# First attention of a four-layer kernel: scores of 16 heads in one block of 32-row products, and one maximum over two banks

## The chip, the cores and the metric

The kernel runs on one core of one Trainium2 chip. The metric is the device time of one execution in microseconds (us), the median of the runs. The engines are named as in the profile: PE is TensorE, PEld its weight loads, DVE VectorE, ACT ScalarE, POOL GpSimd, SP SyncE.

## The reference, cut to what matters

The input x has 16 sequences of 128 positions and 128 channels. Four layers follow, each with a conditioned projection, an attention (or a recurrence), a second conditioned step and a feed-forward part. The change touches the attention of the first layer alone:

```
y   = x @ (W_base + 2 * sum_e cond[b, e] * Bs[e] @ As[e]).T + b_base
Q,K = y @ Wq.T, y @ Wk.T          modulated per channel by amplitude and phase
V   = (y + y shifted by one position) @ Wv.T, modulated per channel
for each of 16 heads (8 channels each):
    scores = (cos part of Q . cos part of K + sin part of Q . sin part of K) * 8 ** -0.5
    out    = softmax(scores) @ V
x   = x + out @ Wo.T
```

So a score of one head is a product over 8 channels taken twice, 16 rows of contraction. There is no causal mask in this layer. The attention of the last layer is built by the same helper (`mh_attn` with `i == 3`) and keeps its order.

## The kernel before, in words

Everything is recorded as a list of steps (`step`, in `order`), and then each engine walks the list and issues its part of each step, so the list sets the order on every engine. `in_order` makes the list: items are sequences of stages, and in every round it starts one new item and moves all live items one stage on, the newest first. A `Ring` gives out buffers and notes which signals its next user must wait for.

The 2048 positions are worked on in four quarters of four sequences (`n`). For each quarter come the conditioned projection into Y (`cw_scale`, `cw`, `cw_add`, `cx`), the products for Q and K (`qk`, two each, modulated by VectorE in `qk_mod`), and V (`v_shift`, `v`, `v_out`). A quarter has four sequences (`j`, the text's step of 128 queries), and a sequence has two halves of 8 heads each. For each half the stages are these:

- scores (`scores`): TensorE multiplies Q and a masked copy of K, in which each head has its own 128 columns and all other heads' rows are zero (`kb`, made by GpSimd, four multiplications for both halves). Rows 0 to 63 hold four heads and rows 64 to 127 four more, so there are two products of 64 rows and 512 columns, one per bank. The four banks 0 to 3 (`RA`) hold two halves, and also take the results of all projections.
- softmax (`rowmax`, `exp`): VectorE takes the maxima of each bank (two reductions, line 2321), subtracts in the first bank into a buffer (line 2324); ScalarE takes the exponentials of the second bank itself, in four operations (line 2027), and then those of the buffer (line 2031).
- transposition (`turn`): TensorE turns the eight 128x128 blocks through banks 4 and 5 (`RB`), ScalarE copies them out (line 2036).
- the product with V (`pv`, lines 1714 and 1718, the second for the sums, both halves with the odd one) into banks 6 and 7 (`RC`).
- norm (`norm`, lines 2330 and 2332): a reciprocal and a multiplication, once per sequence, as a stage of its own.

At the end of a quarter `att_out` multiplies by Wo (line 1745) and VectorE adds into X (line 2335). Beside the heads GpSimd mixes the second conditioning weights (lines 2800 and 2804), and VectorE quantizes feed-forward weights (`fq`) and picks the experts (`top_index`, line 2261).

The order of a quarter's items, with the next quarter's projections among the heads, is one line:

```
out_items += (hd[0:1] + scale + hd[1:2] + product + hd[2:3] + out + q + hd[3:4] + k + hd[4:5] + v + hd[5:8])
```

## Time and profile before

| | before |
|---|---|
| median of 3 runs | 1345.44 us (1345.07 to 1346.12) |
| the profiled execution | 1353.68 us |
| its span, first to last instruction | 1351.9 us |
| PE busy | 1222.1 us (90%) |
| PEld busy | 960.2 us (71%) |
| DVE busy | 830.8 us (61%) |
| ACT busy | 653.7 us (48%) |
| POOL busy | 285.1 us (21%) |
| mean granted clock of PE | 0.979 |

The first attention lies in the first eighth of the span: its first score product starts at 24.98 us, its last addition into X at 164.31 us. A share of busy time is a mean over stages with different limits; the text below reads it stretch by stretch. A duration in the timeline runs to an instruction's end; since instructions of one engine overlap, the distance from one start to the next is shorter, and both are used.

### The profile page before, as it was taken

The numbers are of one execution on the slowest core, as the hardware profiler recorded it, in microseconds if no ns is written. First come the engines' busy times: TensorE is split into PE (matmuls) and PEld (weight loads), VectorE is DVE, ScalarE is ACT, GpSimd is POOL, SyncE is SP. The second block draws the span as 40 slices with busy tenths as digits, with TensorE's granted clock in tenths as the row PEclk, the third lists the DMA queues.
The fourth block names the chain that finished last, engine by engine and source line by source line (L and its number), as shares of the span: only waits on it lengthen the run. The fifth ranks groups of instructions, "written<-read, shape, count | busy, mean of one in ns | idle before, by whom it ended". The sixth has DMA issues, their size and how long they took to land.

```text
span 1351.9 us, 27707 instructions
## 1 busy us (share of the span) xinstructions
PE 1222.1 (90%) x10063; PEld 960.2 (71%) x10063; DVE 830.8 (61%) x1781; ACT 653.7 (48%) x1338; POOL 285.1 (21%) x381
## 2 busy tenths in 40 slices
PE   5999971889999899999999999889999999989999
PEld 2555620458788889887887888478889866657777
DVE  4888678564555566657777565456564477764242
ACT  2666686445434334444454444233434457755553
POOL 4877300120003142330000014043340021200000
PEclk9999995999999999999999999999999999999999
DMA  9000010501142113103106101032102000000000
GB/s 326 2 1 2 11 69 0 210 1 63 35 177 84 56 53 102 49 27 147 67 1 249 68 7 48 24 101 67 47 18 87 1 2 2 3 2 1 1 16 16
DMA packets 42898, 75.86 MB, mean 56 GB/s; under 512 B 3848, under 2 KB 33680, under 8 KB 41872
## 3 DMA queue, kind: packets, MB, share of 16 engines
q1 hardware_dynamic: 38672, 65.69, 13.4%
q0 software_dynamic: 4096, 8.40, 2.1%
q8 instruction: 86, 1.41, 0.4%
q14 instruction: 44, 0.36, 0.1%
HBM read 59.78 MB, written 14.29 MB: 55 GB/s over the span
## 4 chain that ended last, share of the span: by engine, by line
PE 76%; DVE 13%; ACT 5%; issue 3%; DVEq 1%; DMA 1%; POOL 0%; ACTq 0%; SPq 0%; POOLq 0%
PE bank L1869 7%; PE bank L1880 7%; PE bank L1865 7%; PE bank L1924 5%; PE bank L1611 4%; PE bank L1856 4%; PE bank L1934 3%; PE bank L1616 3%; PE bank L1618 3%; PE bank L1617 3%; PE bank L1681 2%; PE bank L1849 2%; PE bank L1851 2%; PE bank L1850 2%; PE bank L1697 2%
## 5 line engine op out<-in xcount | busy, mean ns | idle before, releaser
L2127 ACT ACTIVATE SC<-bank 128x512 f32<-128x512 f32 x192 | 114.3, 595 | 223.1 <-PE bank L1865 124.0
L2214 DVE SCALAR_TENSOR_TENSOR SC<-bank,SM,SC 128x512 f32<-128x512 f32 x128 | 95.8, 748 | 123.2 <-PE bank L1869 102.5
L1880 PE MATMUL bank<-A,SC 128*128 x1024 | 137.0, 277 | 7.9 <-DVE SC L2214 7.1
L1869 PE MATMUL bank<-X,SC 128*128 128x128 f32 x1024 | 136.8, 277 | 4.4 <-DVE SC L2489 3.9
L1865 PEld LDWEIGHTS bank<-X,SC 128*128 128x128 f32 x1024 | 126.1, 192 | 20.0 <-issue 13.0
L1865 PE MATMUL bank<-X,SC 128*128 128x128 f32 x1024 | 136.1, 276 | 3.7 <-ACT SC L2111 2.5
L1880 PEld LDWEIGHTS bank<-A,SC 128*128 128x128 f32 x1024 | 125.4, 192 | 17.4 <-issue 16.5
L1869 PEld LDWEIGHTS bank<-X,SC 128*128 128x128 f32 x1024 | 124.5, 192 | 6.9 <-DVE SC L2489 6.7
L1924 PE MATMUL bank<-A 128*128 128x128 f32 x736 | 100.4, 280 | 16.0 <-DVE A L2639 10.5
L1924 PEld LDWEIGHTS bank<-A 128*128 128x128 f32 x736 | 90.1, 193 | 21.1 <-ACT A L2152 13.0
L2790 POOL TENSOR_SCALAR A<-A,CC 128x256 f32<-128x256 f32 (+1 forms) x128 | 55.4, 451 | 189.7 <-DVE A L2306 102.2
L2111 ACT ACTIVATE SC<-A 128x512 f32 x128 | 80.6, 629 | 28.5 <-PE bank L1869 23.0
L2840 POOL DMA_INDIRECT A<-ys,POSI x64 | 62.5, 976 | 133.1 <-PE bank L1918 37.9
L2828 POOL DMA_INDIRECT xs<-CC,POSI x64 | 63.7, 996 | 119.3 <-DVE POSI L2618 28.1
L2027 ACT ACTIVATE A<-bank,SM 128x128 f32<-128x128 f32 (+1 forms) x256 | 70.3, 371 | 37.2 <-DVE SM L2321 37.1
L2469 DVE TENSOR_TENSOR SC<-bank,SC 128x512 f32<-128x512 f32 x64 | 44.3, 692 | 62.4 <-PE bank L1851 49.1
L2321 DVE TENSOR_REDUCE SM<-bank 128x4 f32<-128x512 f32 (+1 forms) x128 | 73.3, 614 | 7.8 <-PE bank L1681 3.8
L1934 PE MATMUL bank<-BW,A 128*128 x552 | 77.1, 277 | 0.0
L1616 PE MATMUL bank<-R 128*128 128x512 f32 x176 | 69.8, 396 | 7.0 <-DVE SC L2214 5.5
L2815 POOL TENSOR_TENSOR SM<-SM 128x32 f32<-128x32 f32 x32 | 8.3, 259 | 315.3 <-DVE SM L2214 313.4
L1934 PEld LDWEIGHTS bank<-BW,A 128*128 128x128 f32 x552 | 70.0, 194 | 1.9 <-issue 1.7
L1618 PE MATMUL bank<-R 128*128 128x512 f32 x176 | 68.8, 391 | 0.0
(340 smaller groups left out, 2530.7 us busy)
## 6 DMA issues: line engine op xcount, KB each, us to landing
A<-in_moe SPq DMA_DIRECT2D x36, 768.0 KB, 10.5
A<-xs SPq DMA_DIRECT2D x20, 256.0 KB, 3.7
ys<-A SPq DMA_DIRECT2D x20, 256.0 KB, 2.3
BW<-in_l1f SPq DMA_DIRECT2D x2, 2048.0 KB, 7.3
BW<-in_l2f SPq DMA_DIRECT2D x1, 3456.0 KB, 10.7
BW<-in_l1c SPq DMA_DIRECT2D x1, 3072.0 KB, 16.7
BW<-in_l3f SPq DMA_DIRECT2D x1, 2816.0 KB, 9.8
A<-in_l1c SPq DMA_DIRECT2D x1, 2560.0 KB, 8.7
```

Source lines behind the costliest of these rows:

```text
L1616: e.matmul(o, wh, hi, start=start, stop=False)
L1618: return e.matmul(o, wl, hi, start=False, stop=stop)
L1865: m = e.matmul(at["pg"].ap[:, cut(q)], wx[:, cut(q)], x, start=True, stop=True)
L1869: m = e.matmul(at["pu"].ap[:, cut(q)], wx[:, cut(4 + q)], x, start=True, stop=True)
L1880: m = e.matmul(o, at["h"].ap[:, cut(q)], W[:, bass.ds(r + (1024 + 128 * q), 128)], start=k == 0 and q == 0, stop=k == 1 and q == 3)
L1924: m = e.matmul(at["pa"].ap[:, cut(q)], at["wt"].ap[:, cut(q)], at["x"].ap, start=True, stop=True)
L1934: m = e.matmul(o, at["ht"].ap[:, cut(q)], BW[:, bass.ds(r + (dn + 128 * q), 128)], start=q == 0, stop=q == nk - 1)
L2027: a = e.activation(s[:, k * (4 + r):k * (5 + r)], at["pa"][1].ap[:, k * r:k * r + k], ACT.Exp, bias=at["m"].ap[:, 4 + r:5 + r])
L2111: e.activation(at["wx"].ap[0][:, 0:512], MOE_AT[at["L"]][:, bass.ds(r, 512)], ACT.Identity).then_inc(at["g"][0], 1)
L2127: e.activation(at["h"].ap, at["pg"].ap, ACT.Gelu_apprx_tanh).then_inc(at["gelu"][0], 1)
L2214: return e.scalar_tensor_tensor(out=o, in0=a, scalar=s, in1=b, op0=o1, op1=o2)
L2321: e.tensor_reduce(m[:, 4 * x:4 * x + 4], pa[x], AX, ALU.max, negate=True).then_inc(at["max"][x][0], 1)
```

## The change

Only the first attention changes. The channels are laid out anew: each group of 32 rows now holds four heads, two in its first set of columns and two in its second, so a row group's product has 32 rows and 256 columns. One `scores` step computes all 16 heads of a sequence, eight products, into four banks: bank g takes row group g, in 2 x 256 columns (`b = 256 * half`), and the two softmax stages of a sequence are given banks 0 and 1, and banks 2 and 3 (`pair["pa"][2 * half:2 * half + 2]`). GpSimd's masked copy has two heads per row group and is made by two multiplications over 256 columns, not four, and is half as wide. The maxima of a half's two neighbouring banks are one reduction over 1024 columns; the eight banks are now one tensor for that.

The order changes with it. The scores of a sequence are recorded at the end of the round in which the odd half before it has had its exponentials (`last_of_round`), and take all four banks of `RA`. All other products of the quarters beside heads (conditioning, Q, K, V, output) go to a ring of three banks that the transpositions share (`RB0`: banks 4, 5 and 7), and the product with V has one bank (`RC0`: bank 6). Q's and K's two products are separate steps, each modulated by itself. The norm is recorded in the same stage as the odd half's product with V, one round sooner.

```diff
+last_of_round = []
@@ in_order @@
+        while last_of_round:
+            last_of_round.pop(0)()
@@ build @@
-        bank = [ctx.enter_context(nc.psum_tensor(f"bank{i}", [128, 512], F32)) for i in range(8)]
+        PS = ctx.enter_context(nc.psum_tensor("banks", [128, 4096], F32))
+        bank = [PS[:, 512 * i:512 * i + 512] for i in range(8)]
...
+        RB0, RC0 = Ring([]), Ring([])
+        RB0.slots, RC0.slots = RB.slots + RC.slots[1:], RC.slots[:1]
@@ cond_items @@
+                ring = RA if src_key or n == 0 else RB0
@@ mh_attn, q_k @@
+                    def mm(half, x=x, n=n, u=u, ring=ring):
+                        at = step("qk", n=n, x=x, half=half, y_in=sig[in_key, n], p=ring.take())
...
+                    return [lambda: last_of_round.append(first), second, lambda: turned(1)]
@@ mh_attn, heads @@
+                        def both_scores(n=n, j=j, u=u):
+                            st = chunk[n]
+                            kb, tkb = st["kb", j]
+                            pair["pa"], pair["mm"] = [RA.take() for _ in range(4)], tick("att_mm")
...
+                            if i == 0 and half and both:
+                                last_of_round.append(both.pop(0))
...
+                        def s_pv_norm(s_pv=s_pv, s_norm=s_norm):
+                            s_pv()
+                            s_norm()
+
+                        if i == 0:
+                            stages = [s_pair, s_soft, s_turn, s_pv_norm if half else s_pv]
@@ tensor, scores @@
-                    for x, pa in enumerate(at["pa"]):
-                        rows, a, b = slice(64 * x, 64 * x + 64), 512 * half + 128 * j, 512 * half
-                        m = e.matmul(pa.ap, q[rows, a:a + 128], kb[rows, b:b + 512], start=True, stop=True)
+                    for half in range(2):
+                        for g, pa in enumerate(at["pa"]):
+                            rows, a, b = slice(32 * g, 32 * g + 32), 512 * half + 128 * j, 256 * half
+                            m = e.matmul(pa.ap[:, b:b + 256], q[rows, a:a + 128], kb[rows, b:b + 256], start=True, stop=True)
@@ vector, rowmax @@
-                    for x in range(2):
+                    if "both" in at:
+                        e.tensor_reduce(m, v4(at["both"], 8), AX, ALU.max, negate=True).then_inc(at["max"][0][0], 1)
+                    for x in range(0 if "both" in at else 2):
@@ gpsimd, kb @@
-                    n = 2 if at["i"] == 0 else 1
+                    n, heads, own = (2, 2, c("hm2")) if at["i"] == 0 else (1, 4, hm)
```

Two places show how the order moves. The first is TensorE between two blocks of scores, in the last quarter, where no projections lie between the heads. Before (L1681 scores, L1611 and L1612 transpositions, L1714 and L1718 the product with V and the sums):

```order
L1681 MATMUL bank<-A 128x512 [waits att_kb,att_act,att_vec]
L1681 MATMUL bank<-A 128x512
L1611 MATMUL bank<-CC,A 128x128 [waits att_act]
L1611 MATMUL bank<-CC,A 128x128 x2
L1612 MATMUL bank<-CC,A 128x128
L1611 MATMUL bank<-CC,A 128x128 [waits att_act]
L1611 MATMUL bank<-CC,A 128x128 x2
L1612 MATMUL bank<-CC,A 128x128
L1714 MATMUL bank<-A 32x128 x8
L1718 MATMUL bank<-SC,CC 32x128 x8
L1718 MATMUL bank<-A,CC 32x128 x8
L1681 MATMUL bank<-A 128x512 [waits att_act,att_vec]
```

In the change (L1741 scores, L1671 and L1672 transpositions, L1774 and L1778 the product with V and the sums):

```order
L1671 MATMUL banks<-CC,A 128x128 [waits att_act]
L1671 MATMUL banks<-CC,A 128x128 x2
L1672 MATMUL banks<-CC,A 128x128
L1671 MATMUL banks<-CC,A 128x128 [waits att_act]
L1671 MATMUL banks<-CC,A 128x128 x2
L1672 MATMUL banks<-CC,A 128x128
L1774 MATMUL banks<-SC,A 32x128 x4
L1774 MATMUL banks<-SC,A 32x128 [waits att_act]
L1774 MATMUL banks<-SC,A 32x128 x3
L1778 MATMUL banks<-A,CC 32x128 x8
L1778 MATMUL banks<-SC,CC 32x128 x8
L1741 MATMUL banks<-A 128x256 [waits att_act,att_kb,att_vec]
```

Before, there is a block of scores ahead of each transposition of a half; now the scores of the next sequence stand behind the even half's transposition and the odd half's product with V of the sequence before.

The second is VectorE at the start of a quarter (before: L2227 the scaling of the conditioning weights, L2321 maxima, L2324 subtraction, L2330 and L2332 the norm, L2350 a feed-forward weight operation):

```order
L2227 TENSOR_TENSOR SC<-CC,SM 128x512
L2321 TENSOR_REDUCE SM<-bank 128x4 [waits att_mm,att_act]
L2321 TENSOR_REDUCE SM<-bank 128x4
L2324 TENSOR_TENSOR A<-bank,SM 128x512 [waits att_vec]
L2330 RECIPROCAL A<-bank 128x128 [waits att_mm]
L2332 TENSOR_TENSOR A<-bank,A 128x128 [waits att_vec]
L2350 TENSOR_TENSOR A<-A,SM 128x384 [waits fq]
L2321 TENSOR_REDUCE SM<-bank 128x4 [waits att_mm,att_act]
L2321 TENSOR_REDUCE SM<-bank 128x4
L2324 TENSOR_TENSOR A<-bank,SM 128x512 [waits att_vec]
```

In the change (L2392 and L2394 the norm, L2287 the scaling, L2381 maxima, L2386 subtraction, L2412 the weight operation):

```order
L2392 RECIPROCAL A<-banks 128x128 [waits att_mm]
L2394 TENSOR_TENSOR A<-banks,A 128x128 [waits att_vec]
L2287 TENSOR_TENSOR SC<-CC,SM 128x512
L2381 TENSOR_REDUCE SM<-banks 128x8 [waits att_mm,att_act]
L2386 TENSOR_TENSOR A<-banks,SM 128x512 [waits att_vec]
L2412 TENSOR_TENSOR A<-A,SM 128x384 [waits fq]
L2392 RECIPROCAL A<-banks 128x128 [waits att_mm]
L2394 TENSOR_TENSOR A<-banks,A 128x128 [waits att_vec]
L2381 TENSOR_REDUCE SM<-banks 128x8 [waits att_act]
L2386 TENSOR_TENSOR A<-banks,SM 128x512 [waits att_vec]
```

The norm between the two halves' maxima was that of the last sequence but one, whose product with V stood a round earlier; that norm now stands ahead of the scaling, and between the maxima stands the norm of the last sequence.

## Rows read from the trace of the kernel before

**Rows 1.** The page, part 4: share of the chain that ended last, by engine.
```profile
PE 76%; DVE 13%; ACT 5%; issue 3%; DVEq 1%; DMA 1%; POOL 0%; ACTq 0%; SPq 0%; POOLq 0%
```

**Rows 2.** Stretch, its us, busy PE, PEld, DVE, ACT, POOL: plain step, two quarters.
```profile
128.60:134.78 6.18, 6.18 (x92) 3.94 (x96) 6.15 (x25) 5.29 (x17) 6.02 (x9) 1.00 0.02 4
38.09:73.60 35.51, 32.41 (x384) 19.86 (x381) 31.92 (x53) 22.50 (x60) 29.11 (x34) 1.00 0.01 2
73.60:107.98 34.38, 33.26 (x387) 20.41 (x387) 28.16 (x51) 22.93 (x60) 25.01 (x31) 1.00 0.01 1
```

**Rows 3.** Timeline of TensorE in a plain step: start, us, instructions.
```profile
131.04 0.55 PE L1611 MATMUL bank<-CC,A 128*128 128x128 f32 x3
...
132.06 0.65 PE L1714 MATMUL bank<-A 128*32 128x128 f32 x16
```

**Rows 4.** The chain in order of time, in a plain step: start, us, what.
```profile
134.78 0.57 PE bank L1714 x16
135.36 0.87 PE bank L1718 x32
136.23 1.06 PE bank L1681 x4
```

**Rows 5.** Timeline round a stall: start, us, what, in brackets idle time and releaser.
```profile
50.59 1.54 DVE L2350 TENSOR_TENSOR A<-A,SM 128x768 f32<-128x768 f32 x1
...
52.06 1.27 DVE L2321 TENSOR_REDUCE SM<-bank 128x4 f32<-128x512 f32 x2
...
53.37 1.14 ACT L2027 ACTIVATE A<-bank,SM 128x128 f32<-128x128 f32 x4 [1.27 <-DVE SM L2321]
...
54.65 0.70 PE L1681 MATMUL bank<-A 64*128 64x512 f32 x2 [1.61 <-ACT A L2027]
```

**Rows 6.** The chain in the last attention: its 32-row score products.
```profile
1139.01 1.04 PE bank L1697 x16
```

**Rows 7.** Lines, shapes kept apart, 1050 to 1300 us: VectorE's maxima.
```profile
L2321 DVE TENSOR_REDUCE SM<-bank 128x4 f32<-128x512 f32 x32 | 20.5, 683 | 2.1 <-PE bank L1697 1.9 <-ACT A L2027 0.2
...
L2321 DVE TENSOR_REDUCE SM<-bank 128x4 f32<-128x256 f32 x32 | 12.0, 417 | 1.6 <-PE bank L1697 0.9 <-ACT A L2027 0.6
```

**Rows 8.** Timeline of plain steps and of the end of the attention.
```profile
134.73 0.16 DVE L2272 TENSOR_SCALAR SM<-SM 128x16 f32<-128x16 f32 x1
...
136.10 1.27 DVE L2321 TENSOR_REDUCE SM<-bank 128x4 f32<-128x512 f32 x2
...
137.41 1.14 ACT L2027 ACTIVATE A<-bank,SM 128x128 f32<-128x128 f32 x4 [0.54 <-DVE SM L2321]
...
137.90 0.94 DVE L2330 RECIPROCAL A<-bank 128x128 f32<-128x128 f32 x1
...
138.42 0.65 ACT L2031 ACTIVATE A<-A 128x512 f32<-128x512 f32 x1
...
139.08 1.28 DVE L2321 TENSOR_REDUCE SM<-bank 128x4 f32<-128x512 f32 x2
...
155.16 0.64 PE L1714 MATMUL bank<-SC,A 128*32 128x128 f32 x16
...
156.74 0.96 DVE L2330 RECIPROCAL A<-bank 128x128 f32<-128x128 f32 x1 [2.99 <-PE bank L1718]
```

**Rows 9.** Lines from 35 to 165 us: busy us, mean ns of one.
```profile
L2261 DVE FIND_INDEX8 IDX<-SM,CC 128x8 uint32<-128x8 f32 x16 | 2.2, 154 | 0.0
L2227 DVE TENSOR_TENSOR SC<-CC,SM 128x512 f32<-128x512 f32 x2 | 2.1, 1041 | 0.0
L2006 ACT ACTIVATE Y<-bank,CC 128x512 f32<-128x512 f32 x3 | 2.1, 687 | 2.3 <-PE bank L1639 2.3
```

**Rows 10.** Timeline of the first scores, and of the last addition into X.
```profile
21.51 5.14 POOL L2790 TENSOR_SCALAR A<-A,CC 128x256 f32<-128x256 f32 x8 [16.29 <-DVE A L2214]
...
24.98 3.68 PE L1681 MATMUL bank<-A 64*128 64x512 f32 x8 [3.70 <-POOL A L2790]
...
164.31 0.69 DVE L2335 TENSOR_TENSOR X<-bank,X 128x512 f32<-128x512 f32 x1 [1.22 <-PE bank L1745]
```

More of the change, by code:

```diff
@@ L294, in add @@
                     st["w"] = at["w"]
-                    RA.give(at["pa"], at["sum"])
+                    ring.give(at["pa"], at["sum"])
                 def all3(scale=scale, product=product, add=add):
@@ L328, in mh_attn @@
             RK = Ring([take(wide, "A0") for _ in range(2)])
-            RKB = Ring([take(2 * wide // 2, "A0") for _ in range(3)])
+            RKB = Ring([take(512, "A0") for _ in range(3)])
             RV = Ring([take(2048, "A0") for _ in range(2)])
@@ L350, in q_k, with turned, first @@
                     u = {}
-                    def mm(x=x, n=n, st=st, u=u):
+                    ring = RB0 if n else RA
+                    def mm(half, x=x, n=n, u=u, ring=ring):
+                        at = step("qk", n=n, x=x, half=half, y_in=sig[in_key, n], p=ring.take())
+                        at["mm"] = tick("att_mm")
+                        u["p", half], u["mm", half] = at["p"], at["mm"]
+                    def turned(half, x=x, st=st, u=u, shift=shift, ring=ring):
+                        if half == 0:
+                            st[x] = (RQ if x == "q" else RK).take()
+                        at = step("qk_mod", half=half, p=u["p", half], mm=u["mm", half], dst=st[x])
+                        at["t"] = st["t" + x] = tick("att_vec")
+                        ring.give(at["p"], at["t"])
+                        if half and x == "q":
+                            shift()
+                    def first(x=x, n=n):
                         if n == 0 and x == "q":
@@ L427, in make_kb @@
                     RK.give(st["k"], t)
-            heads = []
+            heads, both, pair = [], [], {}
             for n in range(NC):
@@ L467, in s_turn @@
                                 RPT.slots[2].over = [sig["moe4_over"]]
-                            at = step("turn", s=u["s"], exp=u["exp"], pb=[RB.take() for _ in range(1 if early else 2)],
+                            at = step("turn", s=u["s"], exp=u["exp"], pb=[rb.take() for _ in range(1 if early else 2)],
                                       p=RPT.take(), tr=[], t=[])
@@ L2788, in _ @@
                     w.wait_ge(*at["tk"])
-                    for r in range(4):
-                        i = e.tensor_scalar(kk[:, :, r, :], k[:, :, at["j"], :], hm[:, r:r + 1], 1.0, ALU.mult, ALU.mult)
+                    for r in range(heads):
+                        i = e.tensor_scalar(kk[:, :, r, :], k[:, :, at["j"], :], own[:, r:r + 1], 1.0, ALU.mult, ALU.mult)
                     i.then_inc(at["t"][0], 1)
```

123 lines of the change are left out of this document (71 added, 52 removed).

## The prediction

> **What bounds the kernel now.** I read the chain that ended last, then the busy time of each engine in stretches of the first attention, then the timeline inside one of them. TensorE carries 76% of the chain [rows 1]. In the last quarter of the first attention a step of 128 queries takes 6.18 us and TensorE is busy in all of it; over quarters with projections beside the heads it is busy 33.3 of 34.4 us, VectorE 28.2 and ScalarE 22.9 [rows 2]. So TensorE sets the pace, and the work that the change shrinks is on the path. It can be rebuilt: a transposition of one half takes 1.02 us (131.04 to 132.06) [rows 3], a score product 1.06, the even half's product with V 0.57, the odd one's 0.57 and 0.87 for the sums [rows 4]. Two of each: 2 x 1.06 + 2 x 1.02 + 0.57 + 1.44 = 6.17. Other engines have room because the four score banks hold two halves: one is being written while the other is reduced. Where that cover fails once, the trace shows the price: a 1.54 us operation delays a pair of maxima to 52.06, the exponentials start at 53.37, and the score product that needs their bank starts at 54.65, after 1.61 us of idle TensorE [rows 5].
>
> **The score products.** Removed: per step two blocks of two 64-row products over 512 columns, 2 x 1.06 us. Added: one block of eight 32-row products over 256 columns. The nearest rows are in the last attention: 32-row products of 256 columns, 16 records (eight products) in 1.04 us of the chain, with four row groups in use [rows 6]. They load 64 weight columns, these 128. I take 1.06 us; below it stands the same block without the start after another shape (0.85), above it no overlap of row groups beyond today's two (2.12). So TensorE saves 1.06 us in each of 16 steps: 17.0 us of work.
>
> The Trainium skill (TensorE: Matmul & The Clock Gate, Part 3) gives 3.07 times, not 4, for four row tiles of 32 rows. By that a block would be some 0.1 us longer, an estimate; the rows above show no such loss for half the weight columns.
>
> **The maxima.** 128x256 takes 417 ns and 128x512 683 ns [rows 7], so 128x1024 is 683 + 2 x 266 = 1215 ns. Two in a row take 1.27 to their end and the subtraction starts 1.20 after the first; now it waits for the one just before it, as the multiplication waits for the reciprocal, so 1.25. Bounds: 1.07 (four times the column term only) and 1.37 (two full ones). I count nothing: the maximum reaches ScalarE after 1.26 us against 1.31 before [rows 8].
>
> **What the path becomes.** One block of scores now fills all four banks, and its first product waits until all four are released, the last by the odd half's exponentials. Scores of the next step no longer run beside the softmax of this one. In the new order TensorE does: scores, odd transposition and even V product of the step before, even transposition of this step, odd V product of the step before, next scores. The even transposition needs this step's maximum and exponentials; the norm of the odd V product stands ahead of the next even maximum on VectorE. That closes a loop per plain step: transposition 1.02; odd V product to norm 1.58 (155.16 to 156.74); norm to the next VectorE operation 1.18 (137.90 to 139.08); maximum to ScalarE 1.26; the bank's exponentials 1.01 (137.41 to 138.42); the buffer's exponential 0.65 with 0.14 to TensorE (own end 54.51, product 54.65) [rows 5, 8]. Sum 6.84 us against 6.18: a plain step gets longer by 0.66, though TensorE works only 5.11 in it. The second way round, over the odd half's exponentials, is shorter: they follow the even ones (from 2.6 to 3.6 us behind the scores' start), the buffer's 0.65 and two copies of 0.6, and end with their own 1.14 and 0.14, near 6.5; the scores wait for the V product.
>
> **A quarter with projections.** Zero is the start of its first scores. Norm of the step before to 1.33, then the weights' scaling, 1.04 us each [rows 9], in front of the even maximum: that starts at 2.35, its exponentials at 3.61, and the even transposition at 5.40, after TensorE has idled since 2.65. Odd V product to 7.86, its norm to 9.19, and only behind this norm stands the odd maximum, though its banks were full at 1.1. Odd exponentials at 10.45, second scores at 11.7. There the even exponentials wait behind the new Y tile (0.69 [rows 9]), which needs a product after the odd transposition: exponentials at 15.45, transposition 17.2, first projection at 18.1. Its modulation stands ahead of the odd maximum: 19.9, exponentials 21.1, third scores 22.4. Next maximum 23.8, V projection to 27.7, its spreading ahead of the odd maximum 28.8, exponentials 30.1, fourth scores 31.4. The last step is plain but starts early: 6.7. Quarter: 38.1 us against 34.4 [rows 2], though TensorE's own work falls from 33.3 to about 29.
>
> **The whole.** First scores wait for GpSimd: eight multiplications take 5.14 us and four release them at 24.98 [rows 10]. Now two do, each over the same 256 columns: 1.8 us sooner. The first quarter has no earlier step beside it, and by the same walk its projection for the next block starts at 37.7 instead of 38.09 (the start of the stretch of 35.51 us [rows 2]); the lead is gone. From there 20.0 to the second quarter's first scores, plus 1.5 for the 1.54 us operation that now stands ahead of a maximum and 0.4 for small ones: 59.6. Two quarters of 38.1 with 1.1 of such operations: 136.9. Then three plain steps of 6.84, with eight index searches (154 ns each [rows 9], 1.2) and five small operations (1.37, from 134.73 to 136.10 [rows 8]) in the loop that had cover before: 160.0. After the last scores, by the same durations with two conditioning products of 1.1 ahead of the tail, the last addition into X comes 14.5 later, at 174.5; it is at 164.31 now [rows 10]. Everything behind it only shifts: **+10 us**. GpSimd's 16 x 0.9 us of saved masking is covered (its next consumer is a step away) and costs or gives nothing.
>
> The sum is against the profiled execution (1353.68 us, span 1351.9). The median of the runs is 1345.44, 0.6% less; a difference of 10 us carries over, so **1355.5**. If durations along the loop are off by 3% of some 150 us it moves by 4 to 5; with the bounds of the maximum (0.15 less or 0.12 more, five times a quarter) and of the scores (0.2 less, 1.06 more, where the maximum waits for them, twice a quarter) I give this case 1348 to 1363.
>
> **Rivals.** *A, faster: TensorE stays the bound.* If each step's other work really fills the gaps, the 17.0 us come off, with 1.8 at the start and some 2 back for shape changes: 1329; with half of it lost, 1337. For it: TensorE is 100% busy in the plain steps [rows 2], and VectorE needs only 4.8 us of 6.2 for its heads (1.80 for maxima and subtraction, 136.10 to 137.90, twice, and 1.18 for the norm [rows 8]). It decides if the loop is under about 6.1 us, that is if norms and projections do not stand ahead of maxima in time; against it is the order itself. The Trainium skill (TensorEngine Tiling (Array Packing), Theoretical Speedup) would have it so, up to four times for 32 rows. Chance 0.20.
>
> *B, no change:* the loop binds only in plain steps, and gains in the others pay for it: 1343 to 1348. It needs quarters of 34 to 35 us, 10% under my walk. Chance 0.07.
>
> *C, more than forecast:* the four row groups do not run side by side. Scores take 2.1 us, which the loop feels where a maximum waits for them, twice a quarter, and in the gap before the even transposition hardly: 8 x 1.06 more, 1364. Against it [rows 6]. Chance 0.05, within the slower side.
>
> Against the change speaks also the Trainium skill (Perfetto Trace Analysis, Matmuls): independent products should rotate through PSUM banks, so that one is emptied while the next is computed. The trace agrees in its one stall of 1.61 us [rows 5]; by that rule the sign is as forecast.
>
> **How the numbers follow.** A measurement here tells about 0.2%, 2.7 us, from no change. Forecast 0.68 and C 0.05 are slower: 0.73; B 0.07; A 0.20. The likeliest is 1355.5. The range reaches down into A, to 1336, and up past C to 1365.
>
> **What would show it.** Steps right: score blocks of about 1.06 us, sixteen of them, each waiting for ScalarE or standing right behind the V product; maxima of 1.2 us; TensorE busy about 75% between first scores and last addition, with idle time before the transpositions that waits for the buffer's exponential; plain steps of 6.8 us, quarters of 38. Wrong: plain steps at or under 6.2, TensorE still over 95% busy, or score blocks of 2 us.

## The result and the profile after

The changed kernel is slower: 1362.36 us (median of 4 runs, 1360.28 to 1363.58) against 1345.26 of the kernel before beside it (1343.17 to 1346.12), ratio 1.0126, 95% interval 1.0113 to 1.0139. That is +17 us where +10 had been forecast. The profiled execution took 1361.25 us, its span is 1359.4. Chips differ by some tenths of a per cent (the kernel before took 1344.8 to 1351.9 us beside the experiments), so what follows compares ratios to the kernel before on the same chip. An interval reaches about 0.0014 (2 us) to each side, and the difference of two ratios is uncertain by about 0.002 (2.5 us).

The page of the kernel after, part 1, and the shares of the chain that ended last [rows 1]:

```profile
PE 1210.9 (89%) x10191; PEld 965.7 (71%) x10191; DVE 832.4 (61%) x1749; ACT 654.1 (48%) x1338; POOL 270.9 (20%) x349
...
PE 72%; DVE 15%; ACT 6%; issue 3%; DVEq 1%; DMA 1%; POOL 0%; ACTq 0%; SPq 0%
```

TensorE has 11 us less work and VectorE and ScalarE more of the chain. All of the loss lies in the first attention: its last addition into X begins at 181.76 us, where it was 164.31 [rows 10], 17.45 later. (The two profiled spans differ by 7.5 us alone: from its last addition into X to its end the profiled execution of before took 1187.6 us and that of after 1177.7. It took 1353.68 us in all, 8 more than the median of before. Stages that the change does not touch were slower in it, so the spans are not compared.)

Stretches of the kernel after: a plain step, the second and third quarter, and the last quarter from its first to its last block of scores. The columns are those of [rows 2]: stretch, its us, busy PE, PEld, DVE, ACT, POOL with counts, granted clock of PE, DMA share, GB/s.

```profile
130.96:137.83 6.87, 4.68 (x80) 3.73 (x81) 5.56 (x31) 4.44 (x13) 6.79 (x9) 1.00 0.00 1
59.08:99.72 40.64, 33.10 (x423) 22.94 (x419) 28.11 (x41) 22.84 (x59) 21.96 (x23) 0.92 0.01 1
99.72:137.83 38.11, 29.35 (x419) 20.43 (x416) 29.98 (x75) 21.22 (x56) 20.17 (x22) 1.00 0.01 2
137.83:167.23 29.40, 20.92 (x291) 15.48 (x291) 19.88 (x41) 15.88 (x45) 13.69 (x14) 0.83 0.01 2
```

Against the 6.18 us of a plain step, full of TensorE's work, and quarters of 34.4 to 35.5 [rows 2], no engine is busy throughout now but GpSimd in the plain step, whose results are not waited for. The clock column is new: 0.92 and 0.83 where before it was 1.00. The trace of before has no half clock from 28.54 to 165.08 us; that of after has five stretches of it before 181.76, together 23.9 us.

The plain step on TensorE and VectorE (timeline: start, us, what, in brackets idle time and releaser):

```profile
130.96 1.15 PE L1741 MATMUL banks<-A 32*128 32x256 f32 x16 [1.08 <-DVE A L2386]
...
135.19 1.21 DVE L2381 TENSOR_REDUCE SM<-banks 128x8 f32<-128x1024 f32 x1
...
135.29 0.52 PE L1671 MATMUL banks<-CC,A 128*128 128x128 f32 x3 [2.16 <-ACT A L2091]
...
136.28 0.65 PE L1774 MATMUL banks<-A 128*32 128x128 f32 x16
...
137.18 0.62 PE L1778 MATMUL banks<-A,CC 128*32 128x128 f32 x16
...
137.87 0.96 DVE L2392 RECIPROCAL A<-banks 128x128 f32<-128x128 f32 x1 [0.74 <-PE banks L1778]
```

The block of eight products takes 1.07 us from its start to the transposition behind it (130.96 to 132.03). TensorE then idles 2.16 us for the buffer's exponential, and VectorE's division waits for the sums at 137.87, with the next maximum behind it. Over the attention the waits read so (engine, line, waited for: us, times, longest; 20 to 180 us):

```profile
ACT A L2087 <- DVE SM L2381: 53.9, 20, 9.1
...
DVE A L2392 <- PE banks L1778: 33.3, 16, 3.9
PE banks L1671 <- ACT A L2091: 17.0, 11, 2.5
```

The division (L2392) waits 33.3 us in 16 steps; in the kernel before (L2330) it waited 10.3 us in 7. And the wide maximum, from the lines of VectorE with shapes kept apart:

```profile
L2381 DVE TENSOR_REDUCE SM<-banks 128x8 f32<-128x1024 f32 x32 | 38.9, 1215 | 5.1 <-PE banks L1741 5.1
```

It takes 1215 ns, the number forecast. The last quarter holds what was not forecast:

```profile
147.18 1.17 PE L1741 MATMUL banks<-A 32*128 32x256 f32 x16
...
155.41 0.90 PE L1671 MATMUL banks<-CC,A 128*128 128x128 f32 x3 [4.42 <-ACT A L2096]
...
157.31 1.08 PE L1774 MATMUL banks<-A 128*32 128x128 f32 x16
158.16 1.93 PE L1778 MATMUL banks<-A,CC 128*32 128x128 f32 x32
160.03 1.56 PE L1741 MATMUL banks<-A 32*128 32x256 f32 x16
```

After 4.42 us of idle time the same products as at 136.28 take 1.08 where they took 0.65, and a transposition 0.90 for 0.52. The granted clock (the number behind the five engines) is 0.50 there, which is 1.2 GHz, and 0.59 in the step before:

```profile
143.12:147.18 4.06, 4.06 (x57) 3.12 (x57) 0.90 (x2) 3.54 (x10) 3.90 (x4) 0.59 0.01 2
155.41:160.03 4.62, 4.62 (x57) 3.74 (x57) 0.92 (x2) 2.95 (x8) 0.00 (x0) 0.50 0.01 4
```

### The profile page after: what moved, and what is told of

It reads as the page before. It is cut to its first block, busy times and chain, and to the rows that moved or that the text cites. A ratio compares the mean times of both kernels' runs of the same rounds, so it can differ in the third digit from the quotient of the medians.

```text
span 1359.4 us, 27888 instructions
## 1 busy us (share of the span) xinstructions
PE 1210.9 (89%) x10191; PEld 965.7 (71%) x10191; DVE 832.4 (61%) x1749; ACT 654.1 (48%) x1338; POOL 270.9 (20%) x349
## 4 chain that ended last, share of the span: by engine, by line
PE 72%; DVE 15%; ACT 6%; issue 3%; DVEq 1%; DMA 1%; POOL 0%; ACTq 0%; SPq 0%
PE banks L1929 7%; PE banks L1940 7%; PE banks L1925 7%; PE banks L1984 5%; PE banks L1916 4%; PE banks L1671 4%; PE banks L1994 3%; PE banks L1676 3%; PE banks L1678 3%; PE banks L1677 3%; PE banks L1909 2%; PE banks L1911 2%; PE banks L1910 2%; PE banks L1757 2%; PE banks L1798 2%
## 5 line engine op out<-in xcount | busy, mean ns | idle before, releaser
L2187 ACT ACTIVATE SC<-banks 128x512 f32<-128x512 f32 x192 | 114.3, 595 | 223.1 <-PE banks L1925 125.7
L2274 DVE SCALAR_TENSOR_TENSOR SC<-banks,SM,SC 128x512 f32<-128x512 f32 x128 | 95.9, 749 | 123.2 <-PE banks L1929 99.9
L1940 PE MATMUL banks<-A,SC 128*128 x1024 | 137.1, 277 | 8.3 <-DVE SC L2274 7.7
L1929 PE MATMUL banks<-X,SC 128*128 128x128 f32 x1024 | 136.9, 277 | 4.7 <-DVE SC L2551 4.2
L1925 PEld LDWEIGHTS banks<-X,SC 128*128 128x128 f32 x1024 | 126.2, 192 | 20.0 <-issue 13.0
L1925 PE MATMUL banks<-X,SC 128*128 128x128 f32 x1024 | 136.2, 276 | 3.7 <-ACT SC L2171 2.5
L1940 PEld LDWEIGHTS banks<-A,SC 128*128 128x128 f32 x1024 | 125.5, 192 | 17.8 <-issue 17.0
L1929 PEld LDWEIGHTS banks<-X,SC 128*128 128x128 f32 x1024 | 124.6, 192 | 7.2 <-DVE SC L2551 7.0
L1984 PE MATMUL banks<-A 128*128 128x128 f32 x736 | 100.0, 280 | 10.9 <-DVE A L2701 5.9
L2087 ACT ACTIVATE A<-banks,SM 128x128 f32<-128x128 f32 (+1 forms) x256 | 70.2, 369 | 65.2 <-DVE SM L2381 53.9
L1984 PEld LDWEIGHTS banks<-A 128*128 128x128 f32 x736 | 89.8, 193 | 15.4 <-ACT A L2212 8.8
L2171 ACT ACTIVATE SC<-A 128x512 f32 x128 | 80.6, 630 | 28.9 <-PE banks L1929 23.1
L1671 PE MATMUL banks<-CC,A 128*128 128x128 f32 x360 | 62.8, 292 | 21.9 <-ACT A L2091 17.0
L1994 PE MATMUL banks<-BW,A 128*128 x552 | 77.4, 278 | 0.0
L1671 PEld LDWEIGHTS banks<-CC,A 128*128 128x128 f32 x360 | 41.6, 145 | 44.1 <-ACT A L2091 19.1
```

Source lines behind the costliest of these rows:

```text
L1671: e.transpose(o[:, cut(r)], i[:, cut(r)], ident)
L1925: m = e.matmul(at["pg"].ap[:, cut(q)], wx[:, cut(q)], x, start=True, stop=True)
L1929: m = e.matmul(at["pu"].ap[:, cut(q)], wx[:, cut(4 + q)], x, start=True, stop=True)
L1940: m = e.matmul(o, at["h"].ap[:, cut(q)], W[:, bass.ds(r + (1024 + 128 * q), 128)], start=k == 0 and q == 0, stop=k == 1 and q == 3)
L1984: m = e.matmul(at["pa"].ap[:, cut(q)], at["wt"].ap[:, cut(q)], at["x"].ap, start=True, stop=True)
L1994: m = e.matmul(o, at["ht"].ap[:, cut(q)], BW[:, bass.ds(r + (dn + 128 * q), 128)], start=q == 0, stop=q == nk - 1)
```

## The experiments

Twelve runs, in four rounds. Each row of the table has the ratio to the kernel before with its interval, and where the third and fourth addition into X begin in the profiled run (the fourth ends the attention). Banks matter for the reading: "two and two" gives two rotating banks and two to the products with V, "three and one" three rotating banks and one.

| kernel | ratio | 95% interval | 3rd, us | 4th, us |
|---|---|---|---|---|
| before | 1 | | 143.51 | 164.31 |
| 32-row products alone | 1.0036 | 1.0023 to 1.0049 | 147.31 | 168.12 |
| and finer projection steps | 1.0029 | 1.0020 to 1.0039 | 147.10 | 167.91 |
| and projections on rotating banks, two and two | 1.0066 | 1.0053 to 1.0079 | 154.69 | 175.16 |
| and one maximum over two banks | 1.0076 | 1.0062 to 1.0090 | 152.77 | 173.18 |
| and division ahead, three and one | 1.0143 | 1.0128 to 1.0159 | 151.96 | 181.00 |
| and the four-bank block: the change | 1.0126 | 1.0113 to 1.0139 | 153.82 | 181.76 |
| the change, division late, two and two | 1.0188 | 1.0174 to 1.0202 | 165.09 | 188.85 |

### Undoing parts of the change

The theory was the prediction's: the four-bank block makes scores and softmax take turns, with the division standing ahead of the next maxima. Rivals: only one of the two costs, or the pieces (32 rows, wide maximum) are slow, or the clock is the loss.

**e1_norm_late**: the division one round later, banks two and two.

```
-        RB0.slots, RC0.slots = RB.slots + RC.slots[1:], RC.slots[:1]
+        RB0.slots, RC0.slots = RB.slots, RC.slots
...
-                            stages = [s_pair, s_soft, s_turn, s_pv_norm if half else s_pv]
+                            stages = [s_pair, s_soft, s_turn, s_pv] + [s_norm] * half
```

> The changed kernel with one thing undone: the division stands again one round behind its products instead of right behind them (the second bank goes back from the rotating banks to the products, two and two as before). The score block over four banks stays. Theory 1 (the four-bank block makes scores and softmax take turns, and the division, waiting for the products, stands in front of the next maxima on VectorE): the loss shrinks, since the maxima no longer wait for the sums of the products; 1346 to 1352 us, TensorE's idle time in the first attention down by half and more. Rival (the loss is the four-bank block alone, the place of the division is covered): 1358 to 1362. Theory 2 (a good part of the loss is TensorE's clock): where the idle stretches of more than 2 us go, the granted clock is 1.00, whatever the order.

Measured 1369.45 us, ratio 1.0188: all expectations missed, it is slower than the change. The last quarter did get shorter, 23.8 us between the third and fourth addition (165.09 to 188.85) against 27.9, but the first three quarters took 11 us more. The edit also takes the third rotating bank from the projections, and the profile shows TensorE's transpositions waiting for copies out of those banks (20 to 189 us):

```profile
PE banks L1671 <- ACT A L2096: 13.9, 6, 2.7
```

In the change this wait is 4.4 us, once (155.41). So with the block of four, three and one with the division ahead is better than two and two with the division late, by 8 us.

**e2_scores_by_halves**: two products of each column half per part, two banks, each part in its own round.

```
                             if (n, j, half) == (0, 0, 0):
-                                both.pop(0)()
+                                RA.at = 0
+                            u["pa"], u["mm"] = [RA.take(), RA.take()], tick("att_mm")
+                            step("scores", i=i, j=j, half=half, kb=kb, tkb=tkb, q=st["q"], tq=st["tq"], pa=u["pa"], mm=u["mm"])
...
-                        for g, pa in enumerate(at["pa"]):
+                        for g, pa in zip((2 * part, 2 * part + 1), at["pa"]):
```

> The changed kernel with the scores of a block computed in two parts again (two of the four row tiles, two banks each, the second part in its own round), the 32-row products, the one maximum over two banks, the rotating banks and the place of the division left as changed. Theory 1: the next scores are computed beside the softmax of the last, the loop is TensorE's again: a plain step 6.2 to 6.5 us instead of 6.87, the whole 1343 to 1351. The scores of a part take about 1.05 us (two row tiles at a time). Rival (32-row products or the wide maximum are slow by themselves): 1355 or more.

1363.17 us, 1.0143, on the rival's side. The theory as it stands falls here: scores that can run beside the softmax again give nothing while the division stands ahead.

**e2b_halves_norm_late**: both edits together.

> Both undone: scores in two parts and the division one round later, so that only 32-row products, the one maximum over two banks, and the finer steps of the projections are left of the change. Theory 1: as the kernel before, 1341 to 1348 (VectorE has 0.15 us less per maximum and GpSimd half as many masked copies, which lie beside TensorE). Rival (the 32-row products cost time): a score part takes 1.3 us or more and the whole is above 1350.

1355.04 us, 1.0076: above what the theory expected, and in time on the rival's side, though not by its mechanism, since a part of the scores takes 1.06 us to the next instruction (125.25 to 126.31) and not 1.3. The fourth addition comes 20.4 us behind the third (20.8 in the kernel before, 29.0 in e2). The wait that went is VectorE's, from 20 us to the end of the attention, e2 first, then e2b:

```profile
DVE A L2399 <- PE banks L1785: 35.3, 16, 4.7
```

```profile
DVE A L2399 <- PE banks L1785: 10.1, 6, 3.8
```

The division in its own round mostly finds its sums ready (10.1 us of waiting, as in the kernel before); ahead of the next maximum it makes that maximum wait for them. The two kernels differ by 9 us (1.0143 less 1.0076). They differ in the banks too, three and one against two and two; the division ahead with two and two was not run, so the 9 us belong to both together. The four-bank block costs nothing measurable on top of the division ahead (1.0126 against 1.0143) and 15 us with the division late (1.0188 against 1.0076). I read it so that either is enough to take TensorE's cover; the runs show that the two costs do not add up, not by which path. And 10 us of loss are left with neither.

### The clock in the changed kernel

**e3_fill_idle**: products of the identity that nobody reads, in the idle stretches of eight steps.

```
+                            fill = {2: 3, 3: 2, 6: 2, 7: 2, 10: 2, 11: 2, 12: 4, 13: 1}.get(4 * n + j, 0)
+                            if half == 0 and fill:
+                                at = step("keep_on", n=fill, after=(), pb=RB0.take())
...
```

> The changed kernel with 18 filler products of the identity (into a free rotating bank, nobody reads them) put behind the first-half attention products of eight steps, where TensorE had been idle for 1.5 to 4.4 us; none stands on the path by more than a part of a us. Theory 2: the granted clock stays at 1.00 through the first attention, the stretches at half clock (66, 97, 145, 158 us) go, and the time falls by 4 to 6 us to 1356 to 1358. Rival (the clock falls for another reason, or the slow stretches are not on the path): no change, 1361 to 1363, or up to 2 us more.

1362.61 us, 1.0130 (1.0114 to 1.0145): no change. The clock did rise, from 0.92 to 0.97 over the attention (after, then e3; stretch from 28 us to the fourth addition):

```profile
28.00:181.76 153.76, 120.18 (x1630) 0.92 0.04 12
```

```profile
28.00:181.88 153.88, 131.64 (x1666) 0.97 0.04 11
```

One step got shorter (139.28 to 147.67, 8.39 us, was 9.35), one longer (131.44 to 139.28, 7.84, was 6.87; the clock fell there instead). In the longest one the expectation that fillers stay off the path was wrong: four of them hold TensorE to 154 us, and the output product, on which a maximum depends, starts at 155.67.

```profile
150.34 3.70 PE L1838 MATMUL banks<-CC 128*128 128x512 f32 x8
155.67 1.13 PE L1810 MATMUL banks<-A,CC 128*128 128x512 f32 x2 [1.63 <-ACT A L2101]
```

So these 18 fillers did not pay in this order; whether better placed ones would, and what the falls of the clock cost here, stays open.

### The remaining 10 us: one part at a time on the kernel before

**e5_rows32_alone**: 32-row products, GpSimd's masked copies halved as in the change, and nothing else.

```
-                    for x, pa in enumerate(at["pa"]):
-                        rows, a, b = slice(64 * x, 64 * x + 64), 512 * half + 128 * j, 512 * half
-                        m = e.matmul(pa.ap, q[rows, a:a + 128], kb[rows, b:b + 512], start=True, stop=True)
+                    for c2 in range(2):
+                        for x, pa in enumerate(at["pa"]):
+                            g, a, b = 2 * half + x, 512 * c2 + 128 * j, 256 * c2
+                            rows = slice(32 * g, 32 * g + 32)
+                            m = e.matmul(pa.ap[:, b:b + 256], q[rows, a:a + 128], kb[rows, b:b + 256], start=True, stop=True)
```

> The kernel before with one part of the change: the scores as 32-row products (four products of 256 columns in two of the four row tiles per part, masked copies of 2 x 256 columns from GpSimd instead of 4 x 256), all orders, banks and the two maxima as before. With the scores by halves and the division late, the run before this still lost 10 us, all of it by the third addition into X (+9.3 us) and none in the last quarter (20.4 us against 20.8). Theory 3 (the projections' new steps and banks cost that): this kernel is not slower than before; its first scores come 3 us sooner because GpSimd has half the masked copies to write, so 1341 to 1345. Rival (32-row products cost, for instance through their operands): above 1348.

1349.40 us, 1.0036: the rival's side. The first scores do start sooner (22.34 us for 24.98), the second quarter is the same (69.36 to 103.77, 34.41 us; before 34.37), the products take no longer where the clock is whole (1.13 us for a part in both). The third quarter takes 43.54 us instead of 38.74. Both kernels have the same order, and the same idle time in the same place. Before:

```profile
124.36 1.13 PE L1681 MATMUL bank<-A 64*128 64x512 f32 x4 [1.13 <-ACT A L2027]
125.42 0.55 PE L1611 MATMUL bank<-CC,A 128*128 128x128 f32 x3
...
126.44 1.13 PE L1681 MATMUL bank<-A 64*128 64x512 f32 x4
```

With 32 rows:

```profile
123.37 1.67 PE L1683 MATMUL bank<-A 32*128 32x256 f32 x8 [1.13 <-ACT A L2029]
124.97 0.90 PE L1611 MATMUL bank<-CC,A 128*128 128x128 f32 x3
...
126.87 2.08 PE L1683 MATMUL bank<-A 32*128 32x256 f32 x8
```

1.13 us idle in both, and then the clock is at half in the one and whole in the other. In the ten us up to this block TensorE was as busy in the one as in the other, before first:

```profile
114.36:124.36 10.00, 8.69 (x103) 5.55 (x104) 9.27 (x33) 5.98 (x17) 8.16 (x12) 1.00 0.01 2
```

```profile
113.37:123.37 10.00, 8.70 (x115) 6.74 (x116) 9.28 (x34) 5.99 (x17) 8.10 (x10) 1.00 0.01 2
```

The stretches with the falls in them, with the granted clock behind PE, PEld, DVE, ACT and POOL, before first:

```profile
52.00:60.00 8.00, 6.14 (x76) 3.62 (x76) 8.00 (x14) 5.94 (x19) 7.92 (x10) 1.00 0.01 2
120.00:130.00 10.00, 8.87 (x107) 5.47 (x105) 9.96 (x62) 7.77 (x22) 9.84 (x15) 1.00 0.01 2
```

```profile
52.00:60.00 8.00, 8.00 (x76) 6.19 (x75) 5.61 (x10) 6.67 (x19) 6.75 (x7) 0.57 0.01 2
120.00:130.00 10.00, 8.87 (x59) 6.20 (x58) 9.23 (x60) 7.27 (x20) 9.68 (x12) 0.69 0.01 2
130.00:140.00 10.00, 10.00 (x150) 7.58 (x149) 7.14 (x14) 6.46 (x17) 5.62 (x7) 0.80 0.01 2
```

So the busy column ahead of the fall, 8.69 and 8.70, does not tell which kernel keeps its clock. (That TensorE is busy 8.87 us over 120 to 130 in both says nothing: with 32 rows much of it is at half clock, with 59 products for 107.) At the other fall, near 52 us, the idle times differ: 2.08 us against 1.61 [rows 5].

**e6_finer_steps**: on the last, q and k products one bank and one round at a time (the change's `first`, `second`, `turned`), all on the four score banks (`ring = RA`).

> As the last, and the projections of q and k cut into the change's finer steps (first product at the end of a round, second one round later, one bank each), but all of them still on the four score banks. Theory 3a (the cost is the move to the rotating banks): as the last kernel within 2 us, 1341 to 1346. Theory 3b (the cost is the later place of the steps, q and k standing ready a round later and more rounds in a quarter): 1350 to 1355.

1348.80 us, 1.0029: in the whole the finer steps cost nothing beside e5 (3a's "within 2 us" holds; its absolute number missed by what e5 missed). The parts are not the same, though. Its scores too start behind 1.13 us of idle time (at 126.25), after ten us in which TensorE was busy 8.87, and here the clock stays at 1.00 with 32-row products:

```profile
116.25:126.25 10.00, 8.87 (x112) 6.28 (x110) 8.60 (x28) 5.50 (x15) 6.32 (x8) 1.00 0.01 2
```

The clock of e6 falls once before the last quarter ends, from 52.84 to 59.67 us, after 2.37 us of idle time. Yet its second quarter takes 35.7 us (70.31 to 106.04) where e5 takes 34.4, and its third 41.1 (106.04 to 147.10) where e9 below, with its clock whole and without the finer steps, takes 39.8. So in this execution the finer steps cost about 1.3 us in each of these quarters, and the clock kept in the third hides it. (Its mean granted clock, 0.980, is the highest of its nine runs; the lowest is 0.977, so others of them may have lost it.)

**e7_rotating_banks**: on the last, the change's own choice of ring for projections, conditioning and output, `ring = RB0 if n else RA`, with two rotating banks where the change has three.

> As the last, with the projections, the conditioning products and the output product moved to the two rotating banks, two maxima of one bank each. It differs from the run at 1355.0 by the maxima alone. Theory 3a: 1353 to 1357, the cost comes with this step; TensorE waits 0.25 us and more for copies out of the rotating banks in each round with a projection. Theory 3b: within 2 us of the kernel with the finer steps alone. The one maximum over two banks is worth nothing or up to 2 us: this kernel is 1355 to 1357.

1354.21 us, 1.0066: theory 3a. The move to two rotating banks costs 5 us (1.0066 less 1.0029; 7.3 by the fourth additions). With it TensorE waits for ScalarE's copies (line 2101) in front of the projections, the conditioning and the output products, 2.3 us in all in steps of 0.2 to 0.3; in e6 there is no wait of this kind. One of them:

```profile
80.08 1.12 PE L1714 MATMUL banks<-Y,CC 128*128 128x512 f32 x2 [0.25 <-ACT A L2101]
```

What the move costs in the change itself, with its third rotating bank, was not run. Against e2b, which differs by the maximum alone, it is 1.0066 to 1.0076: one maximum for two is worth nothing measurable.

**e8_rows32_near_max**: e5 with one maximum wherever the two banks taken are neighbours, `RA.take_near()` in place of two `RA.take()`.

> The kernel before with 32-row products and one maximum over two banks wherever the two banks taken are neighbours, two maxima elsewhere; no bank is reserved, no step moved. If theory 3 holds this has what the change can give without what it costs: TensorE bounds it, VectorE has 0.15 us less per part, so as the 32-row kernel or up to 2 us less: 1339 to 1345. Rival (a maximum over two banks comes later than the second of two, and what waits for it loses): 1345 to 1350.

1349.91 us, 1.0033 (1.0021 to 1.0045): in the rival's range, but e5 stands at 1.0036 without the wide maximum, so the level is not the maximum's: again it is worth nothing, and costs nothing. 23 of the 32 maxima were wide, so two banks can mostly be neighbours without the move that costs 5 us.

### Keeping the clock with 32-row products

**e9_rows32_fill**: e5 and three fillers.

```
+                            if half == 0 and 4 * n + j in {2: 2, 10: 1}:
+                                keep_on({2: 2, 10: 1}[4 * n + j])
```

> The kernel with 32-row products alone (1349.4 us), in the order of before, plus three filler products of the identity that nobody reads, in two places where its TensorE was idle: two before the scores at 50.7 us (2.08 us idle there), one before the scores at 123.4 us (1.13 us idle). Behind each of these the granted clock had gone to half (0.57 over 52 to 60 us, 0.69 over 120 to 130), while the kernel before, with 64-row products in the same order and 1.61 and 1.13 us idle at the same places, kept 1.00. Theory 4 (the 32-row products leave TensorE so little busy that a short idle time takes its clock, and this is their whole cost): the clock stays at 1.00, the third addition into X comes at 139 to 142 us instead of 147.3, and the time is 1340 to 1344, below the kernel before, since the first scores come 2.6 us sooner. Rival (the clock falls for another reason, or the fillers push the scores back): 1347 or more.

Ratio 0.9974 (0.9965 to 0.9983): 1348.58 us beside 1351.37 of the kernel before on that chip, which is 1341.9 on the scale of 1345.4; the third addition comes at 141.58 us. Against e5's 1.0036 the three products are worth 8 us by the ratios and 5.7 by the fourth additions (168.12 and 162.40). They stand in the idle time and the scores behind them come on time:

```profile
49.67 1.98 PE L1777 MATMUL bank<-CC 128*128 128x512 f32 x4
51.80 1.13 PE L1685 MATMUL bank<-A 32*128 32x256 f32 x8 [0.16 <-ACT A L2031]
```

```profile
52.00:60.00 8.00, 7.94 (x112) 6.15 (x110) 7.97 (x14) 7.40 (x22) 7.84 (x8) 1.00 0.01 2
120.00:130.00 10.00, 9.93 (x128) 6.93 (x119) 9.97 (x54) 9.49 (x27) 9.77 (x12) 1.00 0.01 2
130.00:140.00 10.00, 9.06 (x151) 7.05 (x151) 9.02 (x16) 6.93 (x21) 9.69 (x9) 1.00 0.01 2
```

The clock is 1.00 throughout, and the third quarter takes 39.78 us instead of 43.54. It is still 1.0 us longer than in the kernel before (38.74); what this version gains over that kernel is the earlier start, with its first addition into X at 67.39 us for 70.40. It beats both kernels.

**e9b_near_max_fill**: the same fillers in e8.

> The same three fillers in the kernel with 32-row products and one maximum wherever two banks are neighbours (1349.9 us). Theory 4: 1339 to 1344, within 1 us of the last kernel (the one maximum is worth nothing where TensorE bounds the loop). Rival: 1347 or more.

Ratio 0.9980 (0.9971 to 0.9989), which is 1342.7 on the scale of 1345.4: as e9.

**e11_before_fill**: the control, the same fillers in the kernel before.

> The kernel before with the same three filler products in the same two places and nothing else. Its clock was 1.00 behind both idle times anyway. Theory 4 (the fillers help the 32-row kernel through the clock alone): nothing to give back here, ratio 0.999 to 1.001, third addition into X at 143 to 144.5 us, clock 1.00 from 44 to 160 us as before. Rival (the fillers help in another way, or the better time of the 32-row kernel with fillers has nothing to do with 32 rows): ratio 0.998 or less.

Ratio 0.9994 (0.9985 to 1.0003), third addition at 144.08 us, clock 1.00: as expected. Fillers do nothing measurable where no clock is lost, so what they gave e5 is the clock.

### The place of the division in the last quarter alone

**e10_norm_late_last**: the change, with e1's two edits from `n == 3` on.

> The changed kernel; in its last quarter alone, where no projections need rotating banks, the division goes back to its own stage and the second bank back to the attention products. Theory 5 (the division in front of the maxima costs where it stands, and giving its bank to the projections is what paid for it in the other quarters): the last quarter, third to last addition into X, takes 23 to 25 us instead of 27.9, and the time is 1357 to 1360. Rival (the place of the division is worth nothing here): 1361 to 1363.

Ratio 1.0154 (1.0140 to 1.0168): neither expectation. The last quarter is shorter, 159.50 to 184.83, 25.3 us instead of 27.9. But the third addition, which falls into the rounds of the fourth quarter, comes at 159.50 instead of 153.82, behind 5.35 us of idle TensorE:

```profile
156.38 1.08 PE L1777 MATMUL banks<-A 128*32 128x128 f32 x16 [5.35 <-ACT A L2099]
```

Of the 5.7 us by which that addition is late, 1.6 were there at the second one already (111.95 for 110.36), in the same order; the rest is this wait for ScalarE's copies, whose cause I did not separate. Theory 5 has its local gain and not its total.

## Why the prediction was right, and where it was not

**How close it was.** +17 us was measured where +10 was forecast. 1362.4 lies inside the case's own 1348 to 1363, at its upper edge, and the size of the loss was put at little more than half.

**TensorE set the pace; score blocks of 1.06, maxima of 1215 ns.** Right: 1.07 to 1.08 us at full clock and 1215 ns. (The 0.85 us at the lower end of the blocks stood in no row, and no block came near it.) Rival C falls with the first. Rivals A and B fall with the loop and the quarters (B needed 34 to 35 us).

**"A plain step gets longer by 0.66", 6.84 us.** Measured 6.87. TensorE works 4.68 in it where 5.11 was said.

**The quarter's walk.** Forecast from the first scores: second scores at +11.7, third +22.4, fourth +31.4, next quarter +38.1. Measured in the second quarter: +12.3, +22.8, +32.3, +40.6; the third quarter took 38.11. The second quarter's first scores were put at 59.6 and came at 59.08, the last quarter's at 136.9 and came at 137.83. That the first of these is so close is in part luck: the start was 1.3 us earlier than forecast, and a stretch at half clock (51.70 to 58.52 us), which the walk did not have, took 4.15 us from 54.93 to 59.08 where the same products take 2.54 at full clock. The tail of 14.5 us measured 14.53.

**"Then three plain steps of 6.84 ... 160.0": the step that failed.** The last block came at 167.23, that is 29.4 us for the 23.1 in the sum. This is 6.3 of the 7 us by which the whole was off. Three terms were missing or too small. TensorE's clock was not in the sum at all: from the even transposition to the next scores it took 4.06 us (143.12 to 147.18) and 4.62 (155.41 to 160.03), where 2.54 stand at full clock (135.29 to 137.83), and the block at 160.03 took 0.4 more: 4.0 together. The five small operations, carried over as 1.37 us, took 3.46 (148.51 to 151.97, shown below). And the transposition at 155.41 waited 0.5 us more for ScalarE's copy out of a rotating bank (its buffer's exponential had ended at 154.87), a wait that the sum had nowhere. By e3 the first of these is an account of where the time lay, not a proof that the whole would be 4 us shorter at full clock.

**"First scores 1.8 us sooner."** They came 3.1 sooner (21.90 for 24.98): GpSimd began at 20.82 instead of 21.51, and two multiplications took 1.08 us to the scores, where four had taken 3.47. The first quarter gave it back as forecast, with the help of the half clock named above.

**"Scores of the next step no longer run beside the softmax of this one": only half the cause.** The number came from a walk that also had the division ahead of the maximum (2.76 of the 6.84 us), and the text gave the loss to the block. The runs share it out otherwise: 32-row products 4 to 5 us, which three fillers at the lost clock give back, and with the finer steps still 4, though then in part through the steps; projections on two rotating banks 5; the division ahead of the maxima 9, together with its three and one banks; the block itself nothing on top. The block costs 15 with the division late, so they are not two costs that add up: either one, as I read the waits, breaks the overlap of softmax and scores. The Trainium skill's advice to rotate independent products through PSUM banks (Perfetto Trace Analysis, Matmuls) fits the pair with the division late (1.0076 against 1.0188), and it is silent in the other pair (1.0143 against 1.0126), where something else holds the pace.

**"GpSimd's 16 x 0.9 us of saved masking is covered", and 32-row products no loss by themselves.** The first was near: beyond the earlier first scores, 1 to 3 us of which e9 keeps, no run shows a gain from it. The second was wrong: in the order of before they came with half clock in two places and cost 4 to 5 us of the whole.

**What stays open.** How much of the change's +17 us the clock holds (23.9 us at half clock do the work of 12 at full, so 12 us at most by TensorE's own work); how the 9 us divide between the place of the division and the banks; why the clock fell in e5 near 124 us, and not in the kernel before at equal idle and busy time, nor in e6, e7 and e2b with 32-row products behind the same 1.13 us (126.25, 133.75 and 130.65): 32 rows alone do not decide it, and nothing here tells what does; and how the 5 us of the rotating banks divide into waits for copies and a longer time at half clock, which that profile also shows (0.78 over 60 to 70 us, where e6 has 1.00). Whether four row tiles in two banks would give both shorter scores and two halves in flight was not tried. The Trainium skill says (TensorEngine Tiling (Array Packing), Gotcha 1: PSUM Pressure) that different row tiles cannot use one PSUM bank at once; no run here shows it. By that rule a block of four row tiles takes four of the eight banks, and that is what makes this change pay with its banks.

## What to carry to other kernels

Before giving work that bounds nothing fewer cycles, count what the new form takes from the schedule: banks that two stages shared, and which instruction now stands ahead of another on the busiest helper engine. Add the parts one at a time, in the old order, and read the granted clock beside each: a part that leaves durations and order alone can still lose through it. Where idle stretches of a us or two are followed by a lower clock, a product that nobody reads, exactly inside the stretch, can give it back; the control without a lost clock shows whether that is the reason.

## What was not expected of the hardware

The clock: at the same place, after the same 1.13 us of idle time and with TensorE busy 8.69 and 8.70 of the 10 us before, 64-row products kept 2.4 GHz and the 32-row products of e5 went to 1.2 GHz. Those of e6, behind 1.13 us too and with 8.87 us busy, kept 2.4 GHz. So rows, idle time and busy time together do not tell. At another place 1.61 us of idle time kept it [rows 5] and 2.08 us with 32-row products did not. Within the changed kernel idle times of 2.17 and 2.16 us (before 104.63 and 135.29) were followed by full clock, and 2.07 us (before 95.63) by 0.72 over 94 to 100 us, so idle time alone does not decide.

Small VectorE operations beside GpSimd: five operations on 16 to 32 columns took 1.37 us in the kernel before, and 3.46 after. Their rows, then GpSimd's at the same time:

```profile
148.51 1.14 DVE L2332 TENSOR_SCALAR SM<-SM 128x16 f32<-128x16 f32 x1
149.69 0.25 DVE L2334 RECIPROCAL SM<-SM 128x16 f32<-128x16 f32 x1
149.98 0.68 DVE L2336 TENSOR_TENSOR SM<-SM 128x16 f32<-128x16 f32 x1
150.69 0.18 DVE L2338 TENSOR_SCALAR SM<-SM 128x32 f32<-128x32 f32 x1
150.91 1.13 DVE L2274 SCALAR_TENSOR_TENSOR SM<-SM 128x32 f32<-128x32 f32 x1
```

```profile
148.35 1.27 POOL L2866 TENSOR_TENSOR A<-A 128x512 f32<-128x512 f32 x1
149.58 1.05 POOL L2862 TENSOR_TENSOR A<-A,CC 128x512 f32<-128x512 f32 x1
150.71 1.29 POOL L2866 TENSOR_TENSOR A<-A 128x512 f32<-128x512 f32 x1
```

The three long ones end at 149.65, 150.66 and 152.04 us, and GpSimd's three at 149.62, 150.63 and 152.00: each waited for the GpSimd operation that had begun before it. The Trainium skill says so (SBUF — State Buffer, SBUF: two separate sides): VectorE operations with two SBUF inputs, or in a two-port mode, and GpSimd operations lock a shared port pair for a whole instruction. The trace agrees for these three; which mode the TENSOR_SCALAR ran in it does not show. The reciprocal at 149.69 took 0.25 us in the middle of a GpSimd operation and did not wait. In the kernel before the three took 0.16, 0.20 and 0.42 us, beside GpSimd multiplications of 0.48 us each: what a small operation ahead of a maximum costs here depends on what GpSimd is doing.
